# Four graph layers on one core: two-half turns and array quarters for the batch jobs of the first two layers

## The chip, the cores and the metric

The kernel runs on one core of one Trainium2 chip. The metric is the device time of one execution in microseconds, taken over several executions of the same program. Times of single instructions come from one further execution, recorded by the hardware profiler. Engines are named as the profile names them: PE is TensorE (PEld its weight loads), DVE VectorE, ACT ScalarE, POOL GpSimd, SP the engine that issues most loads.

## The reference

Four layers over 8 batches of 1024 nodes with 64 features, each of the form x = layernorm(x + layer(x, adj)). The first two layers, which the change is in, are:

```
# layer 1
fa = feat @ W1a.T ; fb = feat @ W1b.T
att[i, j] = sum_o relu(fa[i, o] + fb[j, o]) * W2[o]
att = softmax(att + mask(adj)) ; out = att @ feat
# layer 2
vu = e @ U2 ; iv = e @ W2
scores[i, j] = sum_c leaky(vu[i, c] + iv[j, c], 0.2) * yita[c]
alpha = softmax(where(adj > 0, scores, -1e12))
agg = leaky(alpha @ e)
emb = leaky((agg + (1 + beta) * e) @ linW.T + linb)
```

Layer 3 is a graph attention over columns, layer 4 an attention with eight heads over 128-node blocks of queries. All in float32.

## The kernel before

Both additive layers are one program, `additive_layers`. It has 2 x 8 batches, one after the other (index g, 0 to 7 first layer, 8 to 15 second), each of 8 tiles of 128 query nodes (index k over all 128 tiles, j within a batch), each tile of 16 groups (index p). A group makes hidden units for 8 of the tile's query nodes: four 128x1024 tiles hidden = relu(keys + query), two queries' 64 features on the partitions, each made by one instruction of ACT (L254, one or two of the four) or DVE (L328, the other two or three). PE then sums them over the features with eight matmuls of 32 columns of weights by 512 (L219), four side by side in the array. Every float32 matmul leaves two records in the trace, a transpose one. Hidden tiles live in six slots (SLOTS); DVE and ACT may be six groups ahead of PE.

A finished tile's scores go through: the masked minimum on DVE (L337, here "mask step"), exponentials on ACT (L283), `turn` on PE (L196, eight transposes into the two banks of psT), copies out of psT on ACT and DVE (L289, L344), and `weigh` on PE (L209). All of it is threaded into the groups of the following tiles: the mask step behind DVE's group 5, the exponentials behind ACT's group 7, weigh and turn behind PE's group 4, the copies at group 10. GpSimd makes the masks (L128, L131, L136).

Besides, each batch has jobs on PE, each with a copy behind it, which all go through the single bank psA one after the other. `projection` prepares the next batch: turn_x in two halves (L166, rows of x to columns, 64 partitions), keys in two halves (L169), queries (L172, two matmuls that add up), in the second layer key_rows in two halves (L174). `finishing` ends the batch before: fold (L186), and in the second layer turn_u in two halves (L179) and linear (L182). The tables AHEAD and BEHIND give each job its tile j and its place, 0 for group 4 (behind weigh and turn) and 1 for group 12:

```
AHEAD = {(0, 0): 0, (0, 1): 1, (1, 0): 2, (1, 1): 3, (2, 1): 4, (4, 1): 5, (5, 0): 6}
BEHIND = {(2, 0): 0, (3, 0): 1, (3, 1): 2, (4, 0): 3}
```

ACT copies the jobs' results (L266 to L276), those of place 0 at its group 11, those of place 1 at group 2 of the next tile. DVE has the rest of a batch in `batch_steps`: scale (L349, L351), add_rows (L358, L361, L366), leaky_rows (L371, L374), linear_out (L379, L383), normalise (L388, L392).

`load_constants` loads the weights: `loads` on SP, `more` on ACT's queue once DVE has filled the list `zeros`. Before the first group the jobs of projection(0) run one after the other. What follows the two layers (column_layer, heads_layer) is not touched. Its line L610 is the score matmul of layer 4, which works in pairs on the two halves of the partitions, L626 its weighing, in pieces of 32 partitions by 64 columns.

Of the kernel before, what the change touches and what calls it, by code (L numbers as in the profile page):

```python
# [9 lines left out]
ALU = mybir.AluOpType  # L10
# [25 lines left out]
def additive_layers(nc, adj, X, rest, later, w, buf, small, ident, nb, n):  # L36
# [47 lines left out]
    done = lambda *job: place[job] + 1  # L84

    with ExitStack() as ctx:
# [33 lines left out]
        def _(gp):  # L120
            def make_mask(k):
# [11 lines left out]
                if m % tiles == 0:  # L133
                    gp.wait_ge(aux_out, done("key_rows", k // tiles, 1))
# [18 lines left out]
        def _(pe):  # L153
            def aux(job):
                what, g, i = job
                layer = g // nb
                if place[job]:
                    pe.wait_ge(aux_out, place[job])
                if what == "turn_x":
# [5 lines left out]
                    for t in range(4):  # L165
                        last = pe.transpose(psA[0:C, t * P:(t + 1) * P], rows(g)[:, (4 * i + t) * C:(4 * i + t + 1) * C],  # L166
                                            ident)
                elif what == "keys":
                    last = pe.matmul(psA[:, :], w["b"][layer], xT[:, i * HALF:(i + 1) * HALF], start=True, stop=True)  # L169
                elif what == "queries":  # L170
                    for odd in range(2):
                        last = pe.matmul(psA[:, :], w["a"][layer][:, odd, :], xT[:, odd:n:2], start=odd == 0, stop=odd == 1)  # L172
                elif what == "key_rows":
                    last = pe.matmul(psA[:, :], w["u"], B2[0:C, g % 2, i * HALF:(i + 1) * HALF], start=True, stop=True)  # L174
                elif what == "turn_u":
                    pe.wait_ge(u_ready, g - nb + 1)
                    pe.nop(nofuse=True)
                    for t in range(4):
                        last = pe.transpose(psA[0:C, t * P:(t + 1) * P], y[:, (4 * i + t) * C:(4 * i + t + 1) * C], ident)  # L179
# [45 lines left out]
            for job in projection(0):  # L225
                aux(job)
            for k in range(K + tiles):
                if 2 <= k < K:
                    pe.wait_ge(min_ready, k - 1)
                for p in range(GROUPS):  # L230
                    if k < K:
                        hidden_group(k, p)
                    if p == 4:
# [4 lines left out]
                        for job in aux_jobs(k, 0):  # L238
                            aux(job)
                    if p == 12:  # L240
                        for job in aux_jobs(k, 1):
                            aux(job)

        @block.scalar
        def _(act):
            def hidden_units(k, p):
                g, j = divmod(k, tiles)
                if j == 0 and p == 0:
                    act.wait_ge(aux_out, done("queries", g, 0))
# [7 lines left out]
            def aux(job):  # L257
                what, g, i = job
                half = slice(i * HALF, (i + 1) * HALF)
# [5 lines left out]
                if what == "turn_x":  # L265
                    act.activation(xT[:, half], psA[0:C, :], ACT.Copy).then_inc(aux_out, 1)  # L266
                elif what == "keys":
                    act.activation(B2[:, g % 2, half], psA[:, :], ACT.Copy).then_inc(aux_out, 1)
                elif what == "queries":
                    act.activation(A2[:, g % 2, :], psA[:, :], ACT.Copy).then_inc(aux_out, 1)  # L270
                elif what == "key_rows":
                    if g >= nb + 2:
                        act.wait_ge(mask_ready, (g - 1) * tiles)
                    act.activation(TB[:, g % 2, half], psA[:, :], ACT.Copy).then_inc(aux_out, 1)
                else:
                    act.activation(uT[:, half], psA[0:C, :], ACT.Copy).then_inc(aux_out, 1)  # L276
# [14 lines left out]
            def copy_o(q):  # L291
                g, half = divmod(q, 2)
                act.wait_ge(weighed, 4 * q + 4)
                if g >= 1:
                    act.wait_ge(aux_made, done("fold", g - 1, 0))
# [22 lines left out]
        def _(dve):  # L318
            def hidden_units(k, p):
                g, j = divmod(k, tiles)  # L320
                if j == 0 and p == 0:
                    dve.wait_ge(aux_out, done("queries", g, 0))
# [982 lines left out]
```

## Time and profile before

| | us |
|---|---|
| median of 3 runs | 5732.4 |
| lowest and highest of them | 5729.77, 5737.68 |
| the profiled execution, its own time | 5738.21 |
| its span, first to last instruction | 5736.3 |
| first mask step, last mask step of the two layers | 59.76, 3970.07 |
| PE, DVE, ACT, POOL busy over the span | 5507.1, 5378.4, 5187.1, 905.5 |
| mean granted clock of PE | 0.973 |

Busy times are unions of the instructions of an engine, and neighbouring instructions overlap by some .07 us, so an engine can be busy all the time while it issues at its best rate. A line of groups or of the timeline has first the engine, then the kernel's line, the operation, the tile written and those read. The program's names are shortened there: apsS, apsT, apsO, apsA are psS, psT, psO, psA; a_B and a_A are the keys and queries.

### The profile page before, as it was taken

The page shows a single profiled execution, that of the slowest core. Times are in us where ns is not written, and L with a number is a line of the kernel's source. Part 1 is how long each engine was busy: PE and PEld are TensorE (multiplying, and loading weights), DVE is VectorE, ACT ScalarE, POOL GpSimd, SP SyncE. Part 2 cuts the span into 40 slices and gives each one's busy share as a digit, 9 for nine tenths or more (in the row PEclk, how much of TensorE's full clock was granted, in tenths as well). Part 3 has the DMA queues.
Part 4 walks back from the last instruction along what each step waited for, and adds up shares of the span by engine and source line. Part 5 has one row for each costly group of instructions (what it writes and reads, how often), then busy time and mean ns, then how long its engine had stood idle before and what let it go on. Part 6 is the DMA issues. An engine that isn't in the chain of part 4 may idle for free. (4 is left out here: it accounts for less than half of the span.)

```text
span 5736.3 us, 137991 instructions
## 1 busy us (share of the span) xinstructions
PE 5507.1 (96%) x58164; PEld 2210.2 (39%) x58164; DVE 5378.4 (94%) x8071; ACT 5187.1 (90%) x6137; POOL 905.5 (16%) x890
## 2 busy tenths in 40 slices
PE   8999999999999999999999999998879999999998
PEld 2333333333333333333333333333445454454454
DVE  8999999999999999999999999997669999999998
ACT  8999999999999999999999999996868888888887
POOL 0000000000000011111111111111312222223223
PEclk9999999999999999999999999998879999999999
DMA  1000000000000000000000000000521110111110
GB/s 43 20 16 20 20 17 18 20 20 16 20 20 16 20 20 16 20 16 20 20 16 20 16 20 20 16 20 26 168 70 33 36 33 25 33 36 33 33 29 15
DMA packets 144490, 156.45 MB, mean 27 GB/s; under 512 B 51782, under 2 KB 119110, under 8 KB 143878
## 3 DMA queue, kind: packets, MB, share of 16 engines
q1 hardware_dynamic: 143238, 147.55, 9.2%
q8 instruction: 466, 7.63, 0.6%
q14 instruction: 146, 1.20, 0.1%
q10 hardware_dynamic: 640, 0.07, 0.0%
HBM read 137.10 MB, written 2.10 MB: 24 GB/s over the span
## 5 line engine op out<-in xcount | busy, mean ns | idle before, releaser
L254 ACT ACTIVATE a_hidden<-a_B,a_A 128x1024 f32<-128x1024 f32 x3264 | 3485.4, 1138 | 193.3 <-PE apsS L219 189.3
L328 DVE TENSOR_SCALAR a_hidden<-a_B,a_A 128x1024 f32<-128x1024 f32 x4928 | 3555.4, 791 | 106.3 <-PE apsS L219 86.2
L219 PE MATMUL apsS<-a_hidden,a_w_sel 128*32 128x512 f32 x32768 | 3557.9, 593 | 3.0 <-DVE a_hidden L328 3.0
L219 PEld LDWEIGHTS apsS<-a_hidden,a_w_sel 128*32 128x32 f32 x32768 | 1045.5, 110 | 2412.5 <-issue 2048.8
L610 PE MATMUL m3S<-xT,Q 64*128 64x512 f32 x2048 | 596.7, 657 | 133.8 <-ACT x_even L654 90.4
L626 PE MATMUL m3O<-ZT,Xr 32*64 32x256 f32 x16384 | 579.6, 415 | 4.3 <-DVE ZT L703 4.3
L654 ACT ACTIVATE x_even<-m3S,bias 128x512 f32<-128x512 f32 x684 | 434.3, 689 | 142.8 <-PE m3S L610 120.5
L626 PEld LDWEIGHTS m3O<-ZT,Xr 32*64 32x64 f32 x16384 | 359.8, 142 | 319.0 <-issue 218.5
L703 DVE STREAM_TRANSPOSE ZT<-x_even 128x1024 f32<-128x1024 f32 x342 | 421.6, 1236 | 55.2 <-ACT x_even L663 50.9
L694 DVE CUSTOM_DVE_ANT_0 x_even<-x_even,mask 128x1024 f32<-128x1024 f32 x342 | 440.4, 1322 | 6.4 <-ACT x_even L654 6.3
L663 ACT ACTIVATE x_even<-x_even,low 128x1024 f32<-128x1024 f32 x342 | 394.0, 1152 | 0.0
L128 POOL TENSOR_SCALAR a_mask<-a_adj_in 128x1024 f32<-128x1024 int32 x64 | 90.4, 1413 | 1675.0 <-DVE small L337 1449.1
L131 POOL TENSOR_SCALAR a_mask<-a_adj_in 128x1024 f32<-128x1024 int32 x64 | 91.0, 1422 | 1557.7 <-issue 1557.7
L610 PEld LDWEIGHTS m3S<-xT,Q 64*128 64x128 f32 x2048 | 161.8, 189 | 334.1 <-ACT x_even L654 174.3
L654 ACT ACTIVATE Z<-m3S,bias 128x512 f32<-128x512 f32 x340 | 215.9, 689 | 62.2 <-PE m3S L610 50.9
L703 DVE STREAM_TRANSPOSE ZT<-Z 128x1024 f32<-128x1024 f32 x170 | 210.1, 1236 | 26.0 <-ACT Z L663 23.9
L694 DVE CUSTOM_DVE_ANT_0 Z<-Z,mask 128x1024 f32<-128x1024 f32 x170 | 219.1, 1323 | 0.1
L663 ACT ACTIVATE Z<-Z,low 128x1024 f32<-128x1024 f32 x170 | 195.9, 1152 | 0.0
L136 POOL TENSOR_TENSOR a_mask<-a_mask,a_TB 128x1024 f32<-128x1024 f32 x64 | 172.5, 2696 | 5.9
L337 DVE CUSTOM_DVE_ANT_0 a_Z<-apsS,a_mask 128x1024 f32<-128x1024 f32 x128 | 155.3, 1214 | 5.3 <-PE apsS L219 5.3
L283 ACT ACTIVATE a_Z<-a_Z,small 128x1024 f32<-128x1024 f32 x128 | 145.2, 1134 | 11.4 <-DVE small L337 11.4
L196 PE MATMUL apsT<-ident,a_Z 128*128 128x128 f32 x1024 | 139.8, 279 | 1.8 <-ACT a_Z L283 1.8
(157 smaller groups left out, 3056.2 us busy)
## 6 DMA issues: line engine op xcount, KB each, us to landing
a_adj_in<-adj SPq DMA_DIRECT2D x128, 512.0 KB, 3.6
adj_in<-adj SPq DMA_DIRECT2D x128, 512.0 KB, 4.1
Xr<-x_odd SPq DMA_DIRECT2D x128, 64.0 KB, 2.5
out<-yn SPq DMA_DIRECT2D x64, 32.0 KB, 1.5
x_even<-x SPq DMA_DIRECT2D x1, 256.0 KB, 2.8
wqT<-L_wqT SPq DMA_DIRECT2D x1, 130.0 KB, 4.3
wkT<-L_wkT SPq DMA_DIRECT2D x1, 130.0 KB, 4.4
wvT<-L_wvT SPq DMA_DIRECT2D x1, 130.0 KB, 4.4
```

The lines of the kernel that those rows point to most:

```text
L136: gp.tensor_tensor(mask[:, k % 2, :], mask[:, k % 2, :], TB[:, row, :], ALU.add).then_inc(mask_ready, 1)
L219: last = pe.matmul(psS[k % 2][32 * q:32 * q + 32, h * HALF:(h + 1) * HALF], w["sel"][layer][:, 30 - 2 * p:62 - 2 * p], hidden[:, (k * GROU ...
L254: act.activation(hidden[:, (k * GROUPS + p) % SLOTS, q, :], B2[:, g % 2, :], ACT.Relu, bias=A2[:, g % 2, pair:pair + 1]).then_inc(hid_act, 1)
L283: act.activation(Z, Z, ACT.Exp, bias=lowest(k), scale=-1.0, accum_out=den[:, g % 2, j:j + 1]).then_inc(probs_ready, 1)
L328: dve.tensor_scalar(hidden[:, (k * GROUPS + p) % SLOTS, q, :], B2[:, g % 2, :], A2[:, g % 2, pair:pair + 1], 0.0, ALU.add, ALU.max).then_i ...
L337: dve.tensor_tensor_reduce(out=Z, in0=psS[k % 2][:, :], in1=mask[:, k % 2, :], scale=1.0, scalar=-LOWEST, op0=ALU.add, op1=ALU.min, accum_ ...
L610: last = pe.matmul(psS[(at + e) % 3][:, :], Q[rows, t % 2, h, :], xT[rows, b % 2, half * HALF:(half + 1) * HALF], start=True, stop=True)
L626: last = pe.matmul(psO[C * e:C * e + C, a, 0:32 * HEADS], Xr[rows, b % 2, at * C:(at + 1) * C], ZT[rows, m % 3, at, :], start=step == 0, s ...
L654: act.activation(Z(k, e)[:, half * HALF:(half + 1) * HALF], psS[(4 * k + 2 * half + e) % 3][:, :], ACT.Prelu, bias=bias[:, b % 2, head:hea ...
L663: act.activation(Z(k, e), Z(k, e), ACT.Exp, bias=low[:, k % 4, e:e + 1], scale=-1.0, accum_out=den[:, m % 8, 2 * h + e:2 * h + e + 1]).the ...
L694: dve.tensor_tensor_reduce(out=Z(k, e), in0=Z(k, e), in1=mask[:, m % 2, :], scale=1.0, scalar=-LOWEST, op0=ALU.add, op1=ALU.min, accum_out ...
L703: dve.transpose(ZT[:, m % 3, :, at:at + 32], Z(k, e).rearrange("p (b i) -> p b i", i=32)).then_inc(turned, 1)
```

## The change

The batch jobs are halved in number and laid out anew. turn_x and turn_u turn all eight tiles in one job: tiles 0 to 3 into partitions 0 to 63 of psA, tiles 4 to 7 into partitions 64 to 127, as plain matmuls with the identity instead of transposes. xT and uT become [128, 512]. All weights exist on both halves of the partitions. keys and key_rows become two matmuls, one for each half, into the two banks of psT; queries four matmuls of 64x64 weights and 256 columns, one in each quarter of the array; linear takes its eight tiles in pairs of halves. Since psT is shared with the turn of the tiles, PE waits before those jobs for the copies of the turned tile, and before a turn for the job of group 12. The order of jobs becomes turn_x, queries, keys, key_rows and fold, turn_u, linear; DVE's linear_out moves from group 10 to group 3. w_a needs no zero fill; four more small loads go to ACT's queue and two more to SP's.

```diff
     def projection(g):
-        jobs = [("turn_x", g, 0), ("turn_x", g, 1), ("keys", g, 0), ("keys", g, 1), ("queries", g, 0)]
-        return jobs + ([("key_rows", g, 0), ("key_rows", g, 1)] if g >= nb else [])
+        return [("turn_x", g), ("queries", g), ("keys", g)] + ([("key_rows", g)] if g >= nb else [])
     def finishing(g):
-        return [("fold", g, 0)] + ([("turn_u", g, 0), ("turn_u", g, 1), ("linear", g, 0)] if g >= nb else [])
-    AHEAD = {(0, 0): 0, (0, 1): 1, (1, 0): 2, (1, 1): 3, (2, 1): 4, (4, 1): 5, (5, 0): 6}
-    BEHIND = {(2, 0): 0, (3, 0): 1, (3, 1): 2, (4, 0): 3}
+        return [("fold", g)] + ([("turn_u", g), ("linear", g)] if g >= nb else [])
+    AHEAD = {(0, 0): 0, (0, 1): 1, (1, 1): 2, (2, 1): 3}
+    BEHIND = {(2, 0): 0, (3, 0): 1, (3, 1): 2}
...
+    halves = [slice(C * h, C * h + C) for h in range(2)]
...
+            def aux(k, job):
...
+                if what in ("queries", "keys", "key_rows", "linear") and k >= 1:
+                    pe.wait_ge(copied_low, min(k, K))
+                    pe.wait_ge(copied_high, min(k, K))
                 if what == "turn_x":
...
                     for t in range(4):
-                        last = pe.transpose(psA[0:C, t * P:(t + 1) * P], rows(g)[:, (4 * i + t) * C:(4 * i + t + 1) * C],
-                                            ident)
+                        for h, side in enumerate(halves):
+                            last = pe.matmul(psA[side, t * P:(t + 1) * P], rows(g)[:, (4 * h + t) * C:(4 * h + t + 1) * C],
+                                             ident, start=True, stop=True)
                 elif what == "keys":
-                    last = pe.matmul(psA[:, :], w["b"][layer], xT[:, i * HALF:(i + 1) * HALF], start=True, stop=True)
+                    for h, side in enumerate(halves):
+                        last = pe.matmul(psT[:, h * HALF:(h + 1) * HALF], w["b"][layer][side, :], xT[side, :],
+                                         start=True, stop=True)
                 elif what == "queries":
                     for odd in range(2):
-                        last = pe.matmul(psA[:, :], w["a"][layer][:, odd, :], xT[:, odd:n:2], start=odd == 0, stop=odd == 1)
+                        for h, side in enumerate(halves):
+                            last = pe.matmul(psT[halves[odd], h * HALF:h * HALF + HALF // 2], w["a"][layer][side, :],
+                                             xT[side, odd:HALF:2], start=True, stop=True)
...
                 elif what == "linear":
-                    for t in range(tiles):
-                        last = pe.matmul(psA[:, t * C:(t + 1) * C], uT[:, t * P:(t + 1) * P], w["lin"], start=True, stop=True)
+                    for t in range(4):
+                        for h, side in enumerate(halves):
+                            last = pe.matmul(psT[:, h * HALF + t * C:h * HALF + (t + 1) * C], uT[side, t * P:(t + 1) * P],
+                                             w["lin"][side, :], start=True, stop=True)
...
             def turn(k):
...
+                for job in aux_jobs(k, 1):
+                    pe.wait_ge(aux_out, done(*job))
...
                 if what == "turn_x":
-                    act.activation(xT[:, half], psA[0:C, :], ACT.Copy).then_inc(aux_out, 1)
+                    act.activation(xT, psA[:, :], ACT.Copy).then_inc(aux_out, 1)
                 elif what == "keys":
-                    act.activation(B2[:, g % 2, half], psA[:, :], ACT.Copy).then_inc(aux_out, 1)
+                    act.activation(B2[:, g % 2, :], psT[:, :], ACT.Copy).then_inc(aux_out, 1)
...
-                    if (j, p) == (4, 10):
+                    if (j, p) == (4, 3):
                         linear_out(g)
...
-                loads += [(w_b[i][:, 0:C], a[wb]), (w_b[i][:, C:P], a[wb])]
-                more += [(w_a[i][:, 0, 0:C], a[wa]), (w_a[i][:, 1, C:P], a[wa])]
+                loads += [(w_b[i][0:C, 0:C], a[wb]), (w_b[i][0:C, C:P], a[wb])]
+                more += [(w_b[i][C:P, 0:C], a[wb]), (w_b[i][C:P, C:P], a[wb]), (w_a[i][0:C, :], a[wa]), (w_a[i][C:P, :], a[wa])]
```

PE in the first layer, where a batch has begun. Before, tiles j = 1 and 2 (L209 weigh, L196 turn, L169 keys, L186 fold, L172 queries, L219 hidden):

```order
L209 MATMUL apsO<-a_PT,x_even 64x128 x8
L196 MATMUL apsT<-ident,a_Z 128x128 x8
L169 MATMUL apsA<-a_xT,a_w_b 128x512
L219 MATMUL apsS<-a_hidden,a_w_sel 32x512 x64
L169 MATMUL apsA<-a_xT,a_w_b 128x512
L219 MATMUL apsS<-a_hidden,a_w_sel 32x512 x64
L209 MATMUL apsO<-a_PT,x_even 64x128 x8
L196 MATMUL apsT<-ident,a_Z 128x128 x8
L186 MATMUL apsA<-a_fold,a_OT 128x64 x8
L219 MATMUL apsS<-a_hidden,a_w_sel 32x512 x64
L172 MATMUL apsA<-a_xT,a_w_a 128x512 x2
```

With the change, tiles j = 0 and 1 (L170 turn_x, L235 hidden, L179 queries, L225 weigh, L212 turn, L174 keys):

```order
L170 MATMUL apsA<-ident,x_even 64x128 x8
L235 MATMUL apsS<-a_hidden,a_w_sel 32x512 x64
L179 MATMUL apsT<-a_xT,a_w_a 64x256 x4
L235 MATMUL apsS<-a_hidden,a_w_sel 32x512 x64
L225 MATMUL apsO<-a_PT,x_even 64x128 x8
L212 MATMUL apsT<-ident,a_Z 128x128 x8
L235 MATMUL apsS<-a_hidden,a_w_sel 32x512 x64
L174 MATMUL apsT<-a_xT,a_w_b 128x512 x2
```

Five jobs became three: the turn is one block of eight at group 4 of tile 0, queries follow at group 12 and no longer come last, and the keys are one block of two at group 12 of tile 1.

PE in the second layer, where the batch before is finished. Before, tiles j = 3 and 4 (L179 turn_u, L182 linear, L174 key_rows):

```order
L179 MATMUL apsA<-ident,a_y 64x128 x4
L219 MATMUL apsS<-a_hidden,a_w_sel 32x512 x64
L179 MATMUL apsA<-ident,a_y 64x128 x4
L219 MATMUL apsS<-a_hidden,a_w_sel 32x512 x64
L209 MATMUL apsO<-a_PT,x_odd 64x128 x8
L196 MATMUL apsT<-ident,a_Z 128x128 x8
L182 MATMUL apsA<-a_lin_w,a_uT 128x64 x8
L219 MATMUL apsS<-a_hidden,a_w_sel 32x512 x64
L174 MATMUL apsA<-a_B,a_u 128x512
```

With the change, tiles j = 2 and 3 (L200 fold, L183 key_rows, L190 turn_u, L195 linear):

```order
L200 MATMUL apsA<-a_fold,a_OT 128x64 x8
L235 MATMUL apsS<-a_hidden,a_w_sel 32x512 x64
L183 MATMUL apsT<-a_B,a_u 128x512 x2
L235 MATMUL apsS<-a_hidden,a_w_sel 32x512 x64
L225 MATMUL apsO<-a_PT,x_odd 64x128 x8
L212 MATMUL apsT<-ident,a_Z 128x128 x8
L190 MATMUL apsA<-ident,a_y 64x128 x8
L235 MATMUL apsS<-a_hidden,a_w_sel 32x512 x64
L195 MATMUL apsT<-a_lin_w,a_uT 128x64 x8
```

key_rows now comes ahead of turn_u, as one block, and linear at group 12 of tile 3 instead of group 4 of tile 4. Tiles 4 to 7 of a batch have no job left.

ACT at the start of the program. Before:

```order
L781 DMA a_w_a<-L_aT 64x64 x2
L781 DMA a_w_a<-L_gnn_U 64x64 x2
L781 DMA a_w_sel<-L_gnn_W 64x1 x2
L781 DMA a_w_sel<-L_gnn_yita 64x1 x2
L766 UNCONDITIONAL_BRANCH
L244 UNCONDITIONAL_BRANCH
L266 ACT_TABLE_LOAD
L266 ACTIVATE a_xT<-apsA 64x512 x2
L268 ACTIVATE a_B<-apsA 128x512 x2
L270 ACTIVATE a_A<-apsA 128x512
```

With the change:

```order
L798 DMA a_w_b<-L_bT 64x64 x2
L798 DMA a_w_a<-L_aT 64x64 x2
L798 DMA a_w_b<-L_gnn_W 64x64 x2
L798 DMA a_w_a<-L_gnn_U 64x64 x2
L798 DMA a_w_sel<-L_gnn_W 64x1 x2
L798 DMA a_w_sel<-L_gnn_yita 64x1 x2
L783 UNCONDITIONAL_BRANCH
L260 UNCONDITIONAL_BRANCH
L281 ACT_TABLE_LOAD
L281 ACTIVATE a_xT<-apsA 128x512
L285 ACTIVATE a_A<-apsT 128x512
L283 ACTIVATE a_B<-apsT 128x1024
```

Twelve loads stand ahead of the layers instead of eight, and three copies instead of five ahead of the first hidden unit.

## Rows read from the trace of the kernel before

**Rows 1.** The page: costliest groups, and the clock row of the 40 slices

```profile
L328 DVE TENSOR_SCALAR a_hidden<-a_B,a_A 128x1024 f32<-128x1024 f32 x4928 | 3555.4, 791 | 106.3 <-PE apsS L219 86.2
...
PEclk9999999999999999999999999998879999999999
```

**Rows 2.** Windows, one batch each: length, busy PE, PEld, DVE, ACT, POOL, clock

```profile
1034.71:1279.16 244.45, 244.45 (x2280) 82.95 (x2272) 235.13 (x358) 230.04 (x232) 14.48 (x10) 1.00 0.07 19
...
2761.44:3011.20 249.76, 249.76 (x2304) 85.93 (x2300) 246.65 (x355) 237.87 (x244) 36.03 (x18) 1.00 0.06 18
```

**Rows 3.** Timeline of PE, second layer: start, length, instructions merged by line

```profile
2784.74 1.12 PE L169 MATMUL apsA<-a_xT,a_w_b 64*128 64x512 f32 x2
2785.79 13.94 PE L219 MATMUL apsS<-a_hidden,a_w_sel 128*32 128x512 f32 x128
2799.66 1.09 PE L209 MATMUL apsO<-a_PT,x_odd 128*64 128x128 f32 x16
...
2801.61 1.90 PE L186 MATMUL apsA<-a_fold,a_OT 128*128 128x64 f32 x16
...
2817.31 2.06 PE L172 MATMUL apsA<-a_xT,a_w_a 64*128 64x512 f32 x4
...
2835.13 0.60 PE L179 MATMUL apsA<-ident,a_y 128*64 128x128 f32 x4
...
2866.00 2.00 PE L182 MATMUL apsA<-a_lin_w,a_uT 64*128 64x64 f32 x16
...
2929.47 27.67 PE L219 MATMUL apsS<-a_hidden,a_w_sel 128*32 128x512 f32 x256
```

**Rows 4.** Timeline of DVE, the same stretch

```profile
2792.55 1.22 DVE L337 CUSTOM_DVE_ANT_0 a_Z<-apsS,a_mask 128x1024 f32<-128x1024 f32 x1
...
2937.58 0.68 DVE L388 TENSOR_TENSOR a_y<-a_y,a_mv 128x512 f32<-128x512 f32 x1
...
2951.49 1.22 DVE L337 CUSTOM_DVE_ANT_0 a_Z<-apsS,a_mask 128x1024 f32<-128x1024 f32 x1
...
2952.63 10.96 DVE L328 TENSOR_SCALAR a_hidden<-a_B,a_A 128x1024 f32<-128x1024 f32 x12
...
2964.12 17.31 DVE L328 TENSOR_SCALAR a_hidden<-a_B,a_A 128x1024 f32<-128x1024 f32 x26
2981.35 1.21 DVE L337 CUSTOM_DVE_ANT_0 a_Z<-apsS,a_mask 128x1024 f32<-128x1024 f32 x1
```

**Rows 5.** Timeline in layer 4: matmuls side by side

```profile
4599.94 1.55 PE L626 MATMUL m3O<-ZT,Xr 32*64 32x256 f32 x48
...
4601.42 1.13 PE L610 MATMUL m3S<-xT,Q 64*128 64x512 f32 x4
```

**Rows 6.** Timeline of the start

```profile
5.39 1.26 ACTq L781 DMA_DIRECT2D a_w_sel<-L_gnn_yita  x2
...
10.30 1.03 PE L166 MATMUL apsA<-ident,x_even 128*64 128x128 f32 x4 [10.30 <-PEq L427]
...
14.01 2.07 PE L169 MATMUL apsA<-a_xT,a_w_b 64*128 64x512 f32 x2 [0.68 <-ACT a_xT L266]
...
23.97 19.88 ACT L254 ACTIVATE a_hidden<-a_B,a_A 128x1024 f32<-128x1024 f32 x19
```

**Rows 7.** Window and timeline of the end of the second layer

```profile
3970.00:3999.00 29.00, 13.54 (x82) 11.38 (x79) 9.71 (x30) 3.62 (x6) 2.12 (x3) 0.57 0.00 0
...
3970.07 1.23 DVE L337 CUSTOM_DVE_ANT_0 a_Z<-apsS,a_mask 128x1024 f32<-128x1024 f32 x1 [5.30 <-PE apsS L219]
...
3972.72 1.06 PE L196 MATMUL apsT<-ident,a_Z 128*128 128x128 f32 x8 [1.83 <-ACT a_Z L283]
3974.66 1.97 PE L209 MATMUL apsO<-a_PT,x_odd 128*64 128x128 f32 x16 [0.88 <-DVE a_PT L344]
...
3983.64 1.03 PE L179 MATMUL apsA<-ident,a_y 128*64 128x128 f32 x4 [2.58 <-DVE a_y L374]
...
3987.16 3.67 PE L182 MATMUL apsA<-a_lin_w,a_uT 64*128 64x64 f32 x16 [0.68 <-ACT a_uT L276]
```

More of the change, by code:

```diff
@@ L133, in make_mask @@
                 if m % tiles == 0:
-                    gp.wait_ge(aux_out, done("key_rows", k // tiles, 1))
+                    gp.wait_ge(aux_out, done("key_rows", k // tiles))
                 gp.wait_ge(mask_made, m + 1)
@@ L153, in _ @@
         def _(pe):
-            def aux(job):
-                what, g, i = job
+            def aux(k, job):
+                what, g = job
                 layer = g // nb
@@ L178, in aux @@
                     for t in range(4):
-                        last = pe.transpose(psA[0:C, t * P:(t + 1) * P], y[:, (4 * i + t) * C:(4 * i + t + 1) * C], ident)
+                        for h, side in enumerate(halves):
+                            last = pe.matmul(psA[side, t * P:(t + 1) * P], y[:, (4 * h + t) * C:(4 * h + t + 1) * C], ident,
+                                             start=True, stop=True)
                 elif what == "linear":
-                    for t in range(tiles):
-                        last = pe.matmul(psA[:, t * C:(t + 1) * C], uT[:, t * P:(t + 1) * P], w["lin"], start=True, stop=True)
+                    for t in range(4):
+                        for h, side in enumerate(halves):
+                            last = pe.matmul(psT[:, h * HALF + t * C:h * HALF + (t + 1) * C], uT[side, t * P:(t + 1) * P],
+                                             w["lin"][side, :], start=True, stop=True)
                 else:
@@ L225, in _ @@
             for job in projection(0):
-                aux(job)
+                aux(0, job)
             for k in range(K + tiles):
@@ L238, in _ @@
                         for job in aux_jobs(k, 0):
-                            aux(job)
+                            aux(k, job)
                     if p == 12:
                         for job in aux_jobs(k, 1):
-                            aux(job)
+                            aux(k, job)
         @block.scalar
@@ L248, in hidden_units @@
                 if j == 0 and p == 0:
-                    act.wait_ge(aux_out, done("queries", g, 0))
+                    act.wait_ge(aux_out, done("keys", g))
                 if k * GROUPS + p >= SLOTS:
@@ L257, in aux @@
             def aux(job):
-                what, g, i = job
-                half = slice(i * HALF, (i + 1) * HALF)
+                what, g = job
                 if what in ("linear", "fold"):
@@ L273, in aux @@
                         act.wait_ge(mask_ready, (g - 1) * tiles)
-                    act.activation(TB[:, g % 2, half], psA[:, :], ACT.Copy).then_inc(aux_out, 1)
+                    act.activation(TB[:, g % 2, :], psT[:, :], ACT.Copy).then_inc(aux_out, 1)
                 else:
-                    act.activation(uT[:, half], psA[0:C, :], ACT.Copy).then_inc(aux_out, 1)
+                    act.activation(uT, psA[:, :], ACT.Copy).then_inc(aux_out, 1)
             def exponentials(k):
@@ L294, in copy_o @@
                 if g >= 1:
-                    act.wait_ge(aux_made, done("fold", g - 1, 0))
+                    act.wait_ge(aux_made, done("fold", g - 1))
                 act.activation(OT[:, 4 * half:4 * half + 4, :], psO[:, :, :], ACT.Copy).then_inc(o_out, 1)
@@ L321, in hidden_units @@
                 if j == 0 and p == 0:
-                    dve.wait_ge(aux_out, done("queries", g, 0))
+                    dve.wait_ge(aux_out, done("keys", g))
                 if k * GROUPS + p >= SLOTS:
@@ L346, in scale @@
             def scale(g):
-                dve.wait_ge(aux_made, done("fold", g, 0))
+                dve.wait_ge(aux_made, done("fold", g))
                 dve.wait_ge(probs_ready, (g + 1) * tiles)
@@ L354, in add_rows @@
                 if g < nb:
-                    dve.wait_ge(aux_out, done("fold", g, 0))
+                    dve.wait_ge(aux_out, done("fold", g))
                 else:
@@ L369, in leaky_rows @@
             def leaky_rows(g):
-                dve.wait_ge(aux_out, done("fold", g, 0))
+                dve.wait_ge(aux_out, done("fold", g))
                 dve.scalar_tensor_tensor(out=y, in0=y, scalar=GAT_SLOPE, in1=y, op0=ALU.mult,
@@ L433, in _ @@
             dve.tensor_scalar(w["sel"][1], w["sel"][1], GAT_SLOPE - 1.0, None, ALU.mult)
-            dve.tensor_scalar(w["u"], ycol.to_broadcast([C, P]), -GAT_SLOPE, None, ALU.mult)
+            dve.tensor_scalar(w["u"], ycol.to_broadcast([P, P]), -GAT_SLOPE, None, ALU.mult)
             dve.tensor_scalar(w["beta1"], w["beta1"], 1.0, None, ALU.add)
@@ L821, in build @@
             w_sel = [sg("a_w_sel0", [P, 62]), sg("a_w_sel1", [P, 62])]
-            w_a, w_b = [sg(f"a_w_a{i}", [C, 2, P]) for i in range(2)], [sg(f"a_w_b{i}", [C, P]) for i in range(2)]
-            u, lin_w, lin_b, beta = sg("a_u", [C, P]), sg("a_lin_w", [C, C]), sg("a_lin_b", [P, C]), sg("a_beta", [P, 1])
-            ycol, fold = sg("a_ycol", [C, 1]), sg("a_fold", [P, C])
+            w_a, w_b = [sg(f"a_w_a{i}", [P, C]) for i in range(2)], [sg(f"a_w_b{i}", [P, P]) for i in range(2)]
+            u, lin_w, lin_b, beta = sg("a_u", [P, P]), sg("a_lin_w", [P, C]), sg("a_lin_b", [P, C]), sg("a_beta", [P, 1])
+            ycol, fold = sg("a_ycol", [P, 1]), sg("a_fold", [P, C])
             xv = a["x"].rearrange("(t p) c -> p t c", p=P)
```

23 lines of the change are left out of this document (13 added, 10 removed).

## Prediction

> **What bounds the kernel now.** I read four views of the profile in this order. First the costliest groups: DVE and ACT each spend some 3500 us on hidden units (DVE 3555.4, with 106.3 idle before them, 86.2 of that waiting for PE), and the clock row of the page shows how PE runs [rows 1]. Three engines are nearly full, so shares decide nothing; each stretch has to be asked which engine never waits. Second, the windows, cut from one mask step to the mask step a batch later [rows 2]. A first-layer batch takes 244.45 us: PE is busy for all of it, DVE for 235.13, ACT for 230.04. A second-layer batch takes 249.76: PE all of it, DVE 246.65, ACT 237.87. So PE sets the pace in both layers, but in the second DVE has only 3.1 us to give. That is the number on which this forecast turns.
>
> Third, PE's timeline [rows 3]. A printed time runs .07 past the next start, so a block costs its printed time less .07: weigh 1.02 and turn the same, keys half 1.05 (a key_rows half prints the same), fold 1.83, queries 1.99, a turn_u half .53 (turn_x halves print .60 to .63 as well), linear 1.93, and 64 hidden matmuls (128 records) 13.87. A tile with no job is 27.61 + 1.02 + 1.02 = 29.65. A job at group 12 costs .14 more, since it cuts the hidden run in two (2 x 13.87 against 27.61); the first block behind a turn gets .09 back (a turn before a fold or turn_u costs .93).
>
> PE's second-layer batch: 8 x 29.65 = 237.2; turn_x .44 + .70 = 1.14; keys 1.05 + 1.20 = 2.25; queries 2.13; key_rows 2.25; fold 1.74; turn_u 1.14; linear 1.93. Sum 249.8, measured 249.76. A first-layer batch has no key_rows, turn_u and linear: 244.5, measured 244.45. Nothing is missing from this account.
>
> Fourth, DVE's timeline where it doesn't wait [rows 4]. From one mask step to the next, in a tile with no other step, it needs 29.86 (2951.49 to 2981.35). The 12 additions behind the mask step print 10.96, .91 each, the 26 later ones 17.31, .67 each: something slows DVE right behind each mask step, and a faster PE won't change that. With the batch steps, each from its start to the next (recip and scale .83, the two leaky steps 1.38, the two linear steps 1.32, row addition and statistics 2.5, normalise 1.32; [rows 4] show the first of normalise's two), DVE's floor for a second-layer batch is 8 x 29.85 + 7.35 = **246.15**. ACT's is further off by [rows 2] and is left out.
>
> **The change, part by part.**
>
> *keys, key_rows (second layer), two 64-row matmuls side by side.* The nearest row is layer 4's score pair, the same shape in both row halves: 4 records in 1.13 [rows 5], so 1.06. Before 2.25, now 1.06 + .14 = 1.20: saves 1.05 each. Bounds: 1.05 (one record pair, fully overlapped) and 2.10 (no overlap).
>
> *queries, four 64x64 quadrants of 256 columns.* No row has this shape. Nearest are the above pair (twice the columns) and layer 4's weigh, eight-fold split, 48 records of 256 columns in 1.55 [rows 5]. Two passes of half of a 512 pass plus the pipeline's end give .68; bounds .5 (half a pair) and 1.2 (a pair plus its .14). Before 1.99 + .14, now .68 + .14: saves 1.31.
>
> *turn_x, turn_u.* They change from 8 transposes of one record to 8 matmuls of two records, 16 records in column pairs. That is weigh's shape exactly (16 records, 128x64, 128 columns): 1.02 [rows 3]. Before 1.14, now 1.02: saves .12, practically nothing. Only the number of jobs falls. Here a rule speaks against the change. The row first: weigh's 16 records come at .064 each, the transposes' four at .13 each, so column pairs do overlap. The Trainium skill (TensorE: Matmul & The Clock Gate, "The mechanism" under packing small matmuls) says that a weight load overlaps matmuls under way only where its row group differs; column pairs share theirs. By that rule a turn would take 16 x .13 = 2.1, and of the 44.0 below 24.4 would be left. Weigh's row disagrees, so I take 1.02.
>
> *linear.* 16 records of 64 rows, now in row pairs on two banks: between .97 (half of 1.93) and 1.93; I take 1.10, since the pair row overlaps almost fully. Before 1.93, now 1.24: saves .69.
>
> *Waits added.* PE now waits before each of these jobs for both copies of the turned tile, and before a turn for the job in the same banks. Both copies stand at group 10 on ACT and DVE, the job at group 12 on PE, and PE's group 12 needs their hidden units of group 12 anyway; likewise ACT empties the job at group 2 and DVE the linear at group 3, while the turn stands behind group 4. Nothing new waits: cost 0, covered by the hidden groups' own wait. DVE's linear steps move from group 10 to 3 of the same tile, which changes no length. ACT loses halves (fewer, wider copies) and has slack already.
>
> *PE per batch now.* First layer 244.5 - 2.48 = 242.0 (DVE far below). Second layer 249.8 - 2.48 - 1.05 - .12 - .69 = 245.4, under DVE's 246.15. **DVE becomes the bound there**, and .75 us of each batch's PE saving is worth nothing.
>
> *Adding up.* Jobs are heaped in tiles 0 to 3 of a batch, DVE's steps in tiles 2 to 7, so an average is not enough. I step tile by tile with two rules: the mask step starts no earlier than 1.56 after PE has finished the tile (2792.55 [rows 4] against 2790.99, which is the weigh at 2799.66 [rows 3] less five groups of 1.734) and no earlier than the last one plus DVE's work; a turn starts no earlier than 2.65 after the mask step (3970.07 to 3972.72 [rows 7]). For the kernel before, the steps give batches of 244.5 in the first layer, then 246.7, 247.1, 251.1, and from batch 10 on 249.8, as [rows 2] have them. With the new prices: batches 0 to 6 242.0 (7 x 2.48 = 17.4 saved); batch 7, with key_rows, 243.2 (3.5); batch 8 246.1 (1.0, since DVE waits in its first tiles and can't make it up later); batch 9 247.2 (3.9); batches 10 to 14 246.15 (5 x 3.65 = 18.2); batch 15 prepares nothing and is DVE's already: 0. Together **44.0**.
>
> *Start.* From PE's first turn to ACT's first hidden unit 10.30 to 23.97, 13.7 us [rows 6], in which matmuls take twice as long as later (a keys half prints 2.07 instead of 1.12). New chain: turn 1.97 (weigh where it is slow too [rows 7]), copy .65, .1, queries 1.36, copy .65, .1, keys 2.2, copy of 1024 columns 1.1: 8.1, saves 5.5. Against it: four more loads on ACT's queue, two take 1.26 [rows 6], so +2.5, less .5 for the two zero fills of w_a that ACT no longer waits for. Net 3.5 (0 to 6).
>
> *End.* The last turn_u ran 3983.64 to 3987.16 in two halves with a copy each, 3.5 [rows 7]; now 1.97 + .7 = 2.7. linear 3.67 there, now some 2.1. Saves 2.4 (0 to 3).
>
> Sum 44.0 + 3.5 + 2.4 = 49.9. The profiled execution took 5738.2, which gives 5688; it lies 5.8 above the median of the three runs, 5732.4, so the forecast against the median is **5682**.
>
> **The rivals.**
>
> *A, DVE doesn't bind.* If 29.86 holds some hidden waiting for slots, PE's full saving counts: the steps give 57.1 instead of 44.0, time 5669. Against it: in the tile of [rows 4] DVE starts its mask step about 3 us after PE has finished the tile, so it isn't held back. Chance .06.
>
> *B, less is saved.* DVE's tile is 30.0 when it never rests (35.7), or quadrants take 1.2 (38.8), or the start gives nothing: 5687 to 5696. Chance .10; Further off, column pairs alone don't overlap: each of 15 turn_x and 7 turn_u jobs costs 16 x .13 = 2.1; the steps then give 24.4, and start and end 2 less each: about 5706. Weigh's row speaks against it. Chance .03. This is the skill's rule on row groups, named above.
>
> *C, slower: neither halves nor quadrants overlap in these short bursts.* PE then runs twice the records one after the other: turns 16 x .13 = 2.1 instead of 1.1, keys, key_rows, queries and linear as before. The steps give 24 us more than before, start and end 4 more: about 5760. It decides as soon as a turn costs over 2 us and a pair of keys over 2. Against it: [rows 3, 5]. With only the row halves failing, the time is about the same as before, 5730. Chances .02 and .02.
>
> *D, slower by the clock.* In the second layer PE will now wait for DVE in short gaps. Where PE had waited before, in the last 29 us of the two layers, weigh took 1.97 instead of 1.09 as printed [rows 3, 7], and the granted clock was .57 in the mean. If such a state held for one tile in ten of the second layer's last six batches, some 5 x 27.6 = 138 us would be lost: 5820. Against it: the clock row stays at 9 through the first two layers, and gaps of tenths of a microsecond are all that DVE's floor leaves. Chance .02.
>
> **How the numbers follow.** Forecast .75, A .06, B .13, C .04 (half of it no change), D .02. About .2%, 11 us, is what a measurement of this kernel can tell from no change. Faster .94, same .02, slower .04. The range takes in A's end and B's first part: 5669 to 5703.
>
> **What would show it.** In the profile after: keys and key_rows as one block of 4 records near 1.06, queries near .7, turns of 16 records near 1.02, linear near 1.1; first-layer batches of 242.0; second-layer batches of 246.2 in which DVE has almost no idle time and PE has short gaps that end with DVE's hidden units; mask steps 29.85 apart. Wrong would be: second-layer batches at 245.4 (A), a turn of 2 us (C), the clock row below 9 before the last tile (D), or ACT waited for at the new copies.

## The result, and the profile after

The changed kernel takes 5684.7 us (median of 4 runs, 5678.3 to 5686.1) against 5731.1 for the kernel before: ratio .9914, with a 95% interval of .9902 to .9927, so 42 to 56 us less. Measured again beside the experiments it came to 5683.7 against 5729.8, .9916 (.9901 to .9931). The forecast was 5682.

The profiled execution of the changed kernel is one of its fastest, 5678.3. That of the kernel before lies 7 us above its median. The difference of the two profiles, 59.9 us, is therefore larger than that of the medians, 46.4; what belongs to the two changed layers is read from the profiles batch by batch.

The costliest group of DVE and PE's hidden matmuls, on the page of the changed kernel (busy and mean, then idle before them and what ended it; hidden units are L344 now, hidden matmuls L235):

```profile
L344 DVE TENSOR_SCALAR a_hidden<-a_B,a_A 128x1024 f32<-128x1024 f32 x4928 | 3547.3, 795 | 65.5 <-PE apsS L235 52.8
L235 PE MATMUL apsS<-a_hidden,a_w_sel 128*32 128x512 f32 x32768 | 3556.7, 593 | 8.8 <-DVE a_hidden L344 8.6
```

The hidden matmuls in the kernel before:

```profile
L219 PE MATMUL apsS<-a_hidden,a_w_sel 128*32 128x512 f32 x32768 | 3557.9, 593 | 3.0 <-DVE a_hidden L328 3.0
```

DVE's waits for PE fell from 86.2 [rows 1] to 52.8, and PE's for DVE's hidden units rose from 3.0 to 8.6. The first groups of the program have 2.8 of the 3.0 and 3.2 of the 8.6; the rest of the 8.6, eight waits, is new and lies in the second layer. The windows of one batch in each layer and of the end (length, busy PE, PEld, DVE, ACT, POOL, clock) say where:

```profile
1020.77:1262.68 241.91, 241.91 (x2292) 82.39 (x2284) 234.42 (x358) 229.59 (x230) 14.48 (x10) 1.00 0.06 19
2727.29:2973.36 246.07, 245.53 (x2328) 84.07 (x2320) 245.79 (x354) 235.92 (x240) 35.96 (x18) 1.00 0.06 18
3921.39:3944.99 23.60, 8.89 (x89) 7.59 (x86) 9.48 (x29) 3.03 (x5) 1.89 (x3) 0.71 0.00 0
```

Against [rows 2], the first-layer batch is 2.54 us shorter and PE is still busy for all of it. The second-layer batch is 3.69 shorter, DVE is busy for all but .28 us, and PE is not. PE's timeline in such a batch:

```profile
2701.74 1.09 PE L170 MATMUL apsA<-ident,x_odd 128*64 128x128 f32 x16
2702.76 13.94 PE L235 MATMUL apsS<-a_hidden,a_w_sel 128*32 128x512 f32 x128
2716.64 0.68 PE L179 MATMUL apsT<-a_xT,a_w_a 64*64 64x256 f32 x8
...
2747.03 1.13 PE L174 MATMUL apsT<-a_xT,a_w_b 64*128 64x512 f32 x4
...
2779.61 1.13 PE L183 MATMUL apsT<-a_B,a_u 64*128 64x512 f32 x4
...
2796.59 1.09 PE L190 MATMUL apsA<-ident,a_y 128*64 128x128 f32 x16
...
2811.48 1.11 PE L195 MATMUL apsT<-a_lin_w,a_uT 64*128 64x64 f32 x16
...
2917.42 1.92 PE L235 MATMUL apsS<-a_hidden,a_w_sel 128*32 128x512 f32 x16
2919.88 25.96 PE L235 MATMUL apsS<-a_hidden,a_w_sel 128*32 128x512 f32 x240 [0.54 <-DVE a_hidden L344]
```

These answer to [rows 3]: the two keys blocks became one of 1.13, queries fell from 2.06 to .68, linear from 2.00 to 1.11, and the turn with four times the records of a half prints weigh's 1.09. The last line is the new state: late in the batch PE stands for .54 us and what ends it is a hidden unit of DVE. DVE's own timeline there has no gap:

```profile
2914.82 10.97 DVE L344 TENSOR_SCALAR a_hidden<-a_B,a_A 128x1024 f32<-128x1024 f32 x12
2925.71 0.68 DVE L360 COPY a_PT<-apsT 128x512 f32<-128x512 f32 x1
2926.31 17.32 DVE L344 TENSOR_SCALAR a_hidden<-a_B,a_A 128x1024 f32<-128x1024 f32 x26
2943.53 1.22 DVE L353 CUSTOM_DVE_ANT_0 a_Z<-apsS,a_mask 128x1024 f32<-128x1024 f32 x1
```

The lengths are those of [rows 4], and the next mask step starts at 2973.36, 29.83 later. From the mask steps of both traces, the batches from start to start:

| batch | before | after | forecast after |
|---|---|---|---|
| 0 | 241.6 | 238.7 | 2.5 less |
| 1 to 6 | 244.45 | 241.91 | 242.0 |
| 7 | 246.4 | 242.8 | 243.2 |
| 8 | 246.7 | 244.4 | 246.1 |
| 9 | 250.5 | 247.5 | 247.2 |
| 10 to 14 | 249.75 | 246.05 (14: 246.4) | 246.15 |
| first to last mask step | 3910.3 | 3865.1 | 44.0 less; measured 45.3 less |

Batch 0 isn't steady: in the repeat of the changed kernel it took 239.1. PE's first hidden matmuls run at half their later rate (1.06 us in the trace instead of .62), up to 25.3 us into the span here, 26.1 in the repeat and 31.2 in the kernel before.

The start of the changed kernel (against [rows 6]):

```profile
7.44 1.27 ACTq L798 DMA_DIRECT2D a_w_sel<-L_gnn_yita  x2
...
12.87 1.97 PE L170 MATMUL apsA<-ident,x_even 128*64 128x128 f32 x16 [12.87 <-PEq L444]
...
20.56 10.51 ACT L270 ACTIVATE a_hidden<-a_B,a_A 128x1024 f32<-128x1024 f32 x10
```

PE's first turn starts 2.57 later, the chain to the first hidden unit takes 7.7 instead of 13.7, so the hidden units start 3.4 us sooner. The end (against [rows 7]):

```profile
3925.98 1.09 PE L225 MATMUL apsO<-a_PT,x_odd 128*64 128x128 f32 x16 [0.87 <-DVE a_PT L360]
3927.86 1.97 PE L200 MATMUL apsA<-a_fold,a_OT 128*128 128x64 f32 x16 [0.78 <-ACT a_OT L312]
3932.40 1.97 PE L190 MATMUL apsA<-ident,a_y 128*64 128x128 f32 x16 [2.58 <-DVE a_y L390]
3935.06 1.97 PE L195 MATMUL apsT<-a_lin_w,a_uT 64*128 64x64 f32 x16 [0.69 <-ACT a_uT L292]
```

From the last mask step to layer 3's first matmul it was 3998.77 - 3970.07 = 28.7 and is 3944.99 - 3921.39 = 23.6. The sum for the two layers is 45.3 + 3.4 + 5.1 = 53.8 us of the profiles' 59.9. The other 6 lie in layer 3, which isn't changed: from its first matmul to layer 4's first score 258.6 before and 252.8 after, at granted clocks of .81 and .74 in its first two stretches (121 and 140 us) before and .84 and .76 after. From there to the end both take 1479. In the repeat of the changed kernel the end of the second layer took 24.9 instead of 23.6, with fold at 3.22 instead of 1.97 and a granted clock of .64, so these parts carry a microsecond or two that belongs to the execution and not to the kernel.

### The profile page after: what moved, and what is told of

It is laid out like the page before. It is cut to its first block and busy times, and to the rows that moved or that the text cites. A ratio compares the mean times of both kernels' runs of the same rounds, so it can differ in the third digit from the quotient of the medians.

```text
span 5676.5 us, 138460 instructions
## 1 busy us (share of the span) xinstructions
PE 5440.4 (96%) x58420; PEld 2185.1 (38%) x58420; DVE 5369.9 (95%) x8069; ACT 5168.9 (91%) x6089; POOL 910.0 (16%) x890
## 5 line engine op out<-in xcount | busy, mean ns | idle before, releaser
L344 DVE TENSOR_SCALAR a_hidden<-a_B,a_A 128x1024 f32<-128x1024 f32 x4928 | 3547.3, 795 | 65.5 <-PE apsS L235 52.8
L235 PE MATMUL apsS<-a_hidden,a_w_sel 128*32 128x512 f32 x32768 | 3556.7, 593 | 8.8 <-DVE a_hidden L344 8.6
L235 PEld LDWEIGHTS apsS<-a_hidden,a_w_sel 128*32 128x32 f32 x32768 | 1046.0, 110 | 2407.0 <-issue 2051.0
L212 PE MATMUL apsT<-ident,a_Z 128*128 128x128 f32 x1024 | 139.8, 279 | 1.8 <-ACT a_Z L299 1.8
```

The costliest lines, as they stand in the source:

```text
L235: last = pe.matmul(psS[k % 2][32 * q:32 * q + 32, h * HALF:(h + 1) * HALF], w["sel"][layer][:, 30 - 2 * p:62 - 2 * p], hidden[:, (k * GROU ...
L344: dve.tensor_scalar(hidden[:, (k * GROUPS + p) % SLOTS, q, :], B2[:, g % 2, :], A2[:, g % 2, pair:pair + 1], 0.0, ALU.add, ALU.max).then_i ...
```

## The experiments

My theory after the result was that of the forecast: row and column pairs overlap, PE bounds the first layer, DVE's floor the second. The rivals were that the gain comes from fewer blocks and not from pairs, that PE still bounds the second layer with blocks dearer than their rows, and that the added waits matter. Times from mask step to mask step are from the trace. Where an edit doesn't reach a batch its time repeats within .1 us from kernel to kernel, batch 0 excepted, which moved by up to 1.2; whole times of one kernel's executions lie up to 8 us apart. Experiments 1, 2, 3, 5 and 6 have one execution each, so they are read from the batches.

**1. More work for PE, on the changed kernel.** If PE bounds a batch, it must lengthen by what PE is given.

```diff
                 if what == "turn_x":
...
-                    for t in range(4):
+                    for t in [0, 1, 2, 3] * 2:
                         for h, side in enumerate(halves):
```

> The changed kernel with turn_x's 16 records issued twice (same results), +1.02 us of PE work in each of 15 batches. Theory (PE bounds the first layer, DVE's floor of 246.15 the second): batches from mask step to mask step 242.9 in the first layer (241.9 before), batches 10 to 14 about 246.3 instead of 246.05, since PE's own 245.3 + 1.02 only just passes DVE's floor. Rival 1 (PE still bounds both layers, and its new blocks cost .8 us per batch more than their rows say): 247.1 in batches 10 to 14 as well. Rival 2 (DVE or ACT already bounds the first layer too): first-layer batches stay near 241.9.

Batches 4 and 11, as in the windows above:

```profile
1026.75:1269.54 242.79, 242.79 (x2308) 83.27 (x2300) 234.36 (x358) 229.56 (x230) 14.48 (x10) 1.00 0.06 19
2738.03:2984.44 246.41, 246.41 (x2344) 85.08 (x2336) 245.91 (x355) 236.44 (x240) 36.01 (x18) 1.00 0.06 18
```

The 16 records cost .88 in the first layer: PE is its bound. In the second they cost .33, and PE's gaps are gone. So PE had some .5 us to give there, and the bound is DVE's. Both rivals of the expectation fall: neither 247.1 in the second layer nor 241.9 in the first. The 16 records cost .14 less than the 1.02 that I had taken.

**2. The same on the kernel before.** The edit is the same, in the transposes of turn_x.

> The kernel before with turn_x's transposes issued twice, +1.06 us of PE work per batch. Theory (PE bounds both layers there): first-layer batches 244.45 + 1.06 = 245.5, batches 10 to 14 249.76 + 1.06 = 250.8, the whole about 16 us longer. Rival (the second layer was DVE's before already, and its batch fell for another reason): 249.8 unchanged in batches 10 to 14.

```profile
1039.97:1285.29 245.32, 245.32 (x2288) 83.81 (x2280) 235.13 (x359) 230.03 (x232) 14.46 (x10) 1.00 0.06 18
2772.00:3022.62 250.62, 250.62 (x2312) 86.83 (x2308) 247.00 (x354) 237.83 (x244) 36.01 (x18) 1.00 0.06 18
```

Plus .87 in the first layer and plus .86 in the second, and 23 us in the one whole time (5755.4 against 5732.0), of which the first to the last mask step hold 12.3; 7 more lie in layer 4, which the edit doesn't reach. Before the change PE bounded both layers. The size was .2 below what I expected per batch: eight transposes more inside a block cost .11 each, without the start and end of a block.

**3. Less work for DVE, before.** One hidden unit of 64 in each second-layer tile goes from DVE to ACT.

```diff
-    return (2, 3) if g % 2 or g == 8 or (layer and g == 4) else (3,)
+    return (2, 3) if g % 2 or g == 8 or (layer and g in (4, 12)) else (3,)
```

> The kernel before with one more hidden unit of 64 per second-layer tile made by ACT instead of DVE (.67 us less for DVE, 1.04 more for ACT, per tile). Theory: PE bounds, DVE's work doesn't count; batches 10 to 14 stay 249.8, only the last batch, which is DVE's, ends some 3 us earlier; the whole 0 to 5 us shorter. Rival (DVE's length sets the batch): 5 us less in every second-layer batch, 35 us in all. ACT would bound at 8 x 29.7 + 4 = 241.5, so it doesn't.

```profile
2759.51:3009.26 249.75, 249.75 (x2304) 85.94 (x2300) 242.97 (x346) 243.71 (x252) 36.02 (x18) 1.00 0.06 18
```

DVE is busy 3.7 us less and the batch is as long as before. At the edges, batch 9 shortened by .8 and batch 14 by 1.1, and batch 15 grew by 1.5, so the second layer gained .4. The whole took 5735.8 against 5732.0 in one execution each, which says nothing. The last mask step came 1.6 us earlier, but 1.2 of that is batch 0 of the first layer, which the edit doesn't reach; the slow first matmuls ended at 28.7 us instead of 31.2 there. That PE bounds batches 10 to 14 stands; the 3 us that I expected from the last batch didn't come.

**4. Less work for DVE, after.** The same edit on the changed kernel, beside the changed kernel itself.

> The changed kernel again, to have its ratio to the kernel before from the same chip as the next two: .991, by the first measurement.

> The changed kernel with one more hidden unit of 64 per second-layer tile made by ACT instead of DVE. Theory (DVE's floor bounds the second layer): DVE's tile falls from 29.85 to 29.18, and PE becomes the bound again: batches 10 to 14 245.3 instead of 246.05, batch 8 243.1 instead of 244.4, last batch 5 us shorter; the whole about 12 us shorter than the changed kernel, ratio to the kernel before .989. Rival 1 (PE bounds already): no difference. Rival 2 (ACT is nearer its limit than its busy time says): second-layer batches longer than 246.05.

```profile
2723.55:2968.76 245.21, 245.21 (x2324) 84.29 (x2320) 241.64 (x347) 242.21 (x248) 36.02 (x18) 1.00 0.06 19
```

The edit that was worth nothing before now shortens this batch, 11, by .9 us, to 245.2 (expected 245.3 from PE's blocks), and PE is busy for all of it again; batches 10 to 14 take 245.2 to 245.4. DVE's part of a tile, read from its timeline in this kernel:

```profile
2923.00 16.64 DVE L344 TENSOR_SCALAR a_hidden<-a_B,a_A 128x1024 f32<-128x1024 f32 x25
2939.57 1.21 DVE L353 CUSTOM_DVE_ANT_0 a_Z<-apsS,a_mask 128x1024 f32<-128x1024 f32 x1
```

25 additions where there were 26, and the next mask step 29.19 later. Batch 8 takes 243.1, batch 9 245.6 (247.5), and the last one, to its last mask step, 208.3 instead of 209.6. There I had expected 5 us less. From first to last mask step it is 3856.6 against 3865.7, 9 us. The median of four runs is 5672.9 against 5683.7 for the changed kernel on the same chip, 10.8 less, with ranges that don't meet (5670.7 to 5676.8 and 5679.1 to 5686.6). Ratio to the kernel before .9898 (.9884 to .9913). Experiments 1 to 4 together settle who bounds what: the same edit acts on one kernel and not on the other, both ways.

**5. Pairs taken away.** Same instructions, same number and order, but both matmuls of a row pair read the lower half of the array's rows. The kernel then leaves out the upper half's operands: their keys, queries, key rows and linear outputs are computed from the lower half's, and its results are not those of the reference.

```diff
                 elif what == "keys":
                     for h, side in enumerate(halves):
-                        last = pe.matmul(psT[:, h * HALF:(h + 1) * HALF], w["b"][layer][side, :], xT[side, :],
+                        last = pe.matmul(psT[:, h * HALF:(h + 1) * HALF], w["b"][layer][halves[0], :], xT[halves[0], :],
                                          start=True, stop=True)
```

and in the same way in queries, key_rows and linear.

> The changed kernel with both matmuls of each pair in keys, queries, key_rows and linear reading the lower row half of the array (the upper half's keys, queries and rows are then those of the lower: this part of the computation is changed). Same instructions, no row pairs. Theory (the saving comes from pairs of row halves running side by side): keys and key_rows blocks 2.1 instead of 1.06, queries 1.1 instead of .60, linear 1.9 instead of 1.04; first-layer batches 243.4 instead of 241.9, batches 10 to 14 248.8 instead of 246.05, the whole about 32 us longer. Rival (the saving comes from fewer blocks and fewer drains between them, pairs don't matter): blocks within .2 us of the changed kernel's, the whole within 5 us.

```profile
2738.74 1.13 PE L179 MATMUL apsT<-a_xT,a_w_a 64*64 64x256 f32 x8
...
2769.59 1.98 PE L174 MATMUL apsT<-a_xT,a_w_b 64*128 64x512 f32 x4
...
2803.02 1.98 PE L183 MATMUL apsT<-a_B,a_u 64*128 64x512 f32 x4
...
2835.74 2.00 PE L195 MATMUL apsT<-a_lin_w,a_uT 64*128 64x64 f32 x16
```

Each block doubles or nearly so: queries .68 to 1.13, keys and key_rows 1.13 to 1.98, linear 1.11 to 2.00. Batch 4 takes 243.21, batch 11 248.56; first to last mask step 3894.0, 29.0 more than the changed kernel. Start and end give 4.8 more, so layer 3 begins at 3978.8 instead of 3945.0: of the 53.8 us that the change saved, some 34 are gone with the overlap of the row halves alone. The whole took 5712.6, 28 more than the changed kernel's median; I had expected 32. What stays are 20 us: fewer blocks, the accumulated queries gone, the shorter start, and the column halves, which still overlap. No run parts these from each other.

**6. The added wait exposed.** AHEAD alone is changed, so that queries, keys and key_rows stand at group 4 right behind the turn whose copies they must wait for.

```diff
-    AHEAD = {(0, 0): 0, (0, 1): 1, (1, 1): 2, (2, 1): 3}
+    AHEAD = {(0, 0): 0, (1, 0): 1, (4, 0): 2, (5, 0): 3}
```

> The changed kernel with queries, keys and key_rows at group 4, right behind the turn of the same tile, instead of group 12 (tiles 0 to 5). They need psT's banks emptied, and the copies stand at group 10 of ACT and DVE. Theory (group 12 is what makes the added wait free): PE stops behind each turn until DVE has made the hidden units up to its group 10 and copied; how long is how far DVE is ahead: 1 to 3 us for each job in the first layer, and more in the second, where DVE lags by up to 7 us and has nothing to make it up with. First-layer batches 243.5 to 248, second-layer ones 248 to 256; the whole 25 to 100 us longer. Rival (the copies are always done in time, or the six slots hide the stop): less than 3 us longer.

PE's timeline in the second layer, then the windows of batches 4 and 11:

```profile
2955.60 1.09 PE L212 MATMUL apsT<-ident,a_Z 128*128 128x128 f32 x8
2960.86 2.08 PE L174 MATMUL apsT<-a_xT,a_w_b 64*128 64x512 f32 x4 [4.17 <-DVE a_PT L360]
2962.86 28.19 PE L235 MATMUL apsS<-a_hidden,a_w_sel 128*32 128x512 f32 x256
```

```profile
1051.85:1301.37 249.52, 244.97 (x2292) 82.25 (x2284) 234.43 (x358) 229.08 (x230) 14.48 (x10) 0.99 0.06 18
2848.67:3112.32 263.65, 249.63 (x2324) 83.95 (x2320) 247.50 (x355) 236.20 (x240) 36.02 (x18) 0.98 0.06 17
```

The whole took 5878.2, 195 us more than the changed kernel and nearly 150 more than the kernel before. In batch 11 PE stood three times for 4.2 to 5.3 us until DVE had copied, some 14 us, and DVE itself then waited 15.6 us for slots that PE hadn't freed:

```profile
DVE a_hidden L344 <- PE apsS L235: 15.6, 9, 4.7
```

(a line of the waits in that window: us in total, times, longest). Batches came out at 249.5 and 263.7 where 243.5 to 248 and 248 to 256 were expected. The mechanism is the one I stated, its size twice the upper end of my range. The stops in batch 4 were 2.0 and 2.6 us, as expected; those of batch 11 were longer. What I had left out is that PE also worked more slowly behind them: its busy time was 245.0 instead of 241.9 in batch 4 and 249.6 instead of 245.5 in batch 11, at granted clocks of .99 and .98 instead of 1.00. PE's idle and busy time together grew by 7.6 and 17.6 us, which is all that the two batches grew by. DVE's 15.6 us of waits are the same loss seen from DVE; they don't add to it. The change's price of 0 for its waits holds because of where the jobs stand, not because the wait is short.

**7. A version that beats both.** Experiment 4's edit, and eight small loads of second-layer weights moved behind the start.

```diff
-                loads += [(w_b[i][0:C, 0:C], a[wb]), (w_b[i][0:C, C:P], a[wb])]
-                more += [(w_b[i][C:P, 0:C], a[wb]), (w_b[i][C:P, C:P], a[wb]), (w_a[i][0:C, :], a[wa]), (w_a[i][C:P, :], a[wa])]
+                early, on_act = (loads, more) if i == 0 else (later, later)
+                early += [(w_b[i][0:C, 0:C], a[wb]), (w_b[i][0:C, C:P], a[wb])]
+                on_act += [(w_b[i][C:P, 0:C], a[wb]), (w_b[i][C:P, C:P], a[wb]), (w_a[i][0:C, :], a[wa]), (w_a[i][C:P, :], a[wa])]
```

lin_w's two loads go to `later` too, and PE waits for later_loaded before the second layer's turns.

> As the one before, and the second layer's weights for keys, queries and linear loaded with the later loads at tile 4 instead of ahead of the program (8 of 23 small loads). Theory: the first turn starts at 10.3 again instead of 12.87, so 2.5 us less, the second layer as in the run before; about 14.5 us shorter than the changed kernel. Rival (the start waits for x or for the engines' start-up, not for the number of small loads): the first turn stays near 12.9.

```profile
10.27 1.97 PE L171 MATMUL apsA<-ident,x_even 128*64 128x128 f32 x16 [10.27 <-PEq L445]
...
17.96 6.35 ACT L271 ACTIVATE a_hidden<-a_B,a_A 128x1024 f32<-128x1024 f32 x6
```

The first hidden unit starts at 17.96 instead of 20.56, 2.6 sooner, as expected: the start hangs on the number of small loads. The edit takes four from ACT's queue and four from SP's, so it doesn't show which queue holds the start back. Median 5669.7 (5666.8 to 5672.1), 14.0 less than the changed kernel in the same runs, ratio to the kernel before .9891 (.9874 to .9908).

## Why the prediction was right

- *PE's blocks.* The mechanism came as forecast. keys and key_rows 1.06, the turns 1.02: as forecast. linear 1.04 (forecast 1.10). queries .60 to .61 (.68): quadrants overlap as well as pairs do, and the block lies nearer its lower bound. That is most of why the first-layer batch fell by 2.54 instead of 2.48.
- *The turn, rule against row.* 16 records in column pairs took 1.02 us, .064 each, as weigh's row said, and experiment 1 gives .055 for each record added to such a block. Without overlap it would be about .11: experiment 5's keys, with four times the columns and one after the other, take 1.91 for four records where the kernel before took 1.05 for two, so .43 a record. In the trace's single records the two of a column pair start .007 us apart and the pairs .11, and their weight loads start while matmuls on the same rows are under way. By the rule of the Trainium skill (TensorE: Matmul & The Clock Gate, "The mechanism"), weight loads overlap matmuls under way only where the row group differs. This trace doesn't agree. The forecast's .13 for a record without overlap held part of a block's start and end: eight transposes added to blocks cost .11 each (experiment 2), so I estimate a turn without overlap at 1.9 rather than 2.1. No run takes the column pairs away.
- *DVE's floor.* Forecast 246.15, measured 246.05, and PE's waits there end with DVE's hidden units; experiments 1 to 4 show the switch of the bound from both sides. Rival A would have given 245.3 in these batches. It appeared only once DVE's work was cut.
- *The transition.* Batch 8 was forecast at 246.1 and took 244.4, batch 9 at 247.2 and took 247.5. The step-by-step account let DVE fall behind sooner than it did: batch 8 saved 2.3 instead of 1.0. It also had batch 9 of the kernel before at 251.1, where it took 250.5, and batch 9 saved 3.0 instead of 3.9; the two errors mostly cancel. Of the 1.3 us between 44.0 and the 45.3 measured, .4 come from these two batches and .8 from batches 0 to 6, half of it from batch 0.
- *Waits.* Priced at 0, and no wait of the profile after names them; experiment 6 shows what hides them.
- *Start.* Forecast 3.5 net, measured 3.4, though both parts were off, and that they cancel is luck: the chain saved 6.0 (5.5), the added loads cost 2.6 (2.0). ACT's loads did begin .5 earlier without the zero fills, but its last load still came 2.05 later and the first turn 2.57. The .5 between these two isn't explained.
- *End.* Forecast 2.4, measured 5.1 in this profile. turn_u's 2.7 and linear's 2.0 are as forecast; the rest is weigh 1.09 and fold 1.97 where they had been 1.97 and 3.65, with a granted clock of .71 in that stretch instead of .57. This part isn't the change's own work: in the repeat of the changed kernel fold took 3.22 again and the end saved 3.8.
- *Rivals.* B (less is saved) didn't come: DVE's tile took 29.83, queries .61, and the start gave its 3.4. C (nothing overlaps) is refuted by the blocks, and experiment 5 gives part of its price: without row overlap 34 of 53.8 us are gone and the kernel took 5712.6, where the forecast had put "only the row halves failing" at 5730. D (clock) didn't come: the clock row stays at 9 through the two layers, with PE's gaps about half a microsecond.

The whole came to 46.4 us by the medians against 49.9 forecast; the interval of 42 to 56 holds both. The two profiles give 53.8 for the two layers and 6 more in layer 3, without a change there. In the ten profiles layer 3 took 254.8 to 259.2 in the three of the kernel before and its edits and 251.5 to 254.4 in the seven of the changed kernel and its edits, so it is not steady. Why the medians show less than the profiles of the two layers stays open.

## What to carry to other kernels

When several engines are near their limit, write each one's work per period as a sum of start-to-start times from a stretch where it never waits; a saving on the first engine is worth only the distance to the second, and moving a single instruction from the second engine can then pay (10.8 us here) where it paid nothing before. Halves and quarters of the array pay for short auxiliary matmuls, even inside a stream of others. Sharing a buffer to get there is free only if the job stands where its release has necessarily happened; a few groups earlier the same wait cost 195 us, where the whole change had saved 46.

## What the runs showed that I had not expected

- A block of matmuls between hidden groups has a fixed part: 16 records alone cost 1.02, 16 more in the same block .88. Eight transposes more, split over two blocks, cost .87, where two blocks of four had cost 1.14.
- After a stop of 4.2 us (experiment 6) the next keys pair took 2.08 instead of 1.13, and the granted clock over the 5.1 us that followed was .70, a mean of the two levels of 1.2 and 2.4 GHz; it had been 1.00 over 11 us shortly before the stop. After the stops of .5 us in the changed kernel nothing of the kind is seen: its granted clock stays 1.00.
- A long stop of PE costs more than its length. In batch 11 of experiment 6 PE's idle time grew by 13.5 us and its busy time by 4.1, together the 17.6 that the batch grew by.
- DVE's slow stretch behind each mask step, which is part of the floor that now bounds the second layer, lies beside GpSimd's mask work. Twelve additions took 10.95 us beside 4.1 us of GpSimd there, and 8.82 in the first layer beside 1.4; at the .666 of the later 26 they would take 8.0. That GpSimd is the cause is not tested.
